# Three-layer graph convolution with residual and LayerNorm: VectorE's casts written as a maximum with a zero in PSUM, gathers of the later layers paced by TensorE, and some casts and waits moved

## The reference

```python
def conv(h, W, b):
    m = jnp.concatenate([h[dst], h[src], edge_attr], axis=1) @ W + b
    return jax.ops.segment_sum(m, dst, num_segments=n_nodes)
h = relu(conv(x, W1, b1)); h = relu(conv(h, W2, b2)); y = conv(h, W3, b3)
out = layernorm(x + y)
```

## Time and profile before

| | |
|---|---|
| three runs | 2799.05, 2801.68 (median), 2805.03 us |
| the profiled execution's own time | 2796.28 us |
| its span in the trace, mean granted TensorE clock | 2794.5 us, 0.981 |
| layer 0 (batches 0 to 24) | to about 1405 us of the span |
| batch 25 and the halves | about 1405 to 1453 us |
| layer 1 from batch 26, layer 2 | about 1453 to 2092 us, 2092 us to the end |

### The profile page before, as it was taken

How to read it: one execution, slowest core, us unless ns; L and a number is a source line. 1 busy time by engine, 2 the same in 40 slices (tenths; PEclk the granted TensorE clock), 3 DMA queues, 4 the chain that set the end, 5 groups by cost and what they waited for, 6 DMA issues and landing times.

```text
span 2794.5 us, 51850 instructions
## 1 busy us (share of the span) xinstructions
PE 2492.9 (89%) x18243; PEld 1820.8 (65%) x18243; DVE 2057.6 (74%) x4510; ACT 2171.0 (78%) x2972; POOL 1706.8 (61%) x1391
## 2 busy tenths in 40 slices
PE   1599999999999999999978888888887888888887
PEld 0155555556555555556657777877776777777777
DVE  7999999999999999999765555555553555555554
ACT  5799899898888988998517777777775777777776
POOL 5354454454453454554357777777766777777776
PEclk9699999999999999999989999999998999999999
DMA  4443533533534434434548777777775777777774
GB/s 94 126 149 113 180 125 113 189 115 122 179 116 137 167 113 153 151 113 174 193 128 270 250 250 248 244 250 252 246 239 183 246 237 246 237 236 242 241 241 127
DMA packets 257344, 519.32 MB, mean 186 GB/s; under 512 B 153954, under 2 KB 189784, under 8 KB 253889
## 3 DMA queue, kind: packets, MB, share of 16 engines
q1 hardware_dynamic: 152596, 299.50, 32.9%
q10 hardware_dynamic: 57404, 146.14, 13.9%
q0 software_dynamic: 47088, 70.34, 10.0%
HBM read 361.98 MB, written 153.81 MB: 185 GB/s over the span
## 4 chain that ended last, share of the span: by engine, by line
PE 49%; POOL 33%; issue 10%; DVE 5%; ACT 3%; DMA 1%; ACTq 0%; SPq 0%; DVEq 0%; POOLq 0%
POOL far_rows L895 32%; PE ps L1633 14%; PE ps L1604 14%; PE ps L1662 8%; PE ps L1648 3%; PE ps L1681 3%; ACT spread L1050 2%; PE ps L1734 2%; PE ps L1696 1%; PE ps L1699 1%; PE ps L1735 1%; DVE is_key L1274 1%; PE ps L1709 1%; ACT blocks L985 1%; PE ps L1720 1%
## 5 line engine op out<-in xcount | busy, mean ns | idle before, releaser
L895 POOL DMA_INDIRECT far_rows<-parts,far_src x1350 | 1652.2, 1224 | 1039.1 <-issue 368.3
L985 ACT ACTIVATE blocks<-ps 128x505 fp8e4<-128x505 f32 x1875 | 1117.8, 758 | 138.5 <-PE ps L1604 135.7
L1050 ACT CAST spread<-blocks 125x1500 fp32r<-125x1500 fp8e4 x637 | 897.6, 1443 | 250.3 <-PE ps L1648 229.0
L1515 DVE CAST spread<-blocks 125x1500 fp32r<-125x1500 fp8e4 x588 | 570.5, 974 | 606.0 <-PE ps L1648 603.0
L1604 PE MATMUL ps<-is_key,is_low 128*128 128x505 bf16 x1875 | 700.4, 384 | 31.4 <-DMA w_own<-in_L_gnn_W 13.9
L1633 PE MATMUL ps<-blocks,parts 125*128 125x375 fp8e4 x2600 | 719.1, 324 | 4.2 <-ACT blocks L985 2.4
L1274 DVE TENSOR_SCALAR is_key<-from_one,parts 128x500 bf16<-128x500 f16 x1875 | 614.9, 359 | 1.6 <-PE ps L1604 0.9
L1648 PE MATMUL ps<-spread,halves_last 125*128 125x376 f32 x2500 | 499.7, 347 | 87.5 <-ACT spread L1050 83.9
L1648 PEld LDWEIGHTS ps<-spread,halves_last 125*128 125x128 f32 x2500 | 422.5, 191 | 137.1 <-ACT spread L1050 128.1
L1633 PEld LDWEIGHTS ps<-blocks,parts 125*128 125x128 bf16 x2600 | 255.1, 99 | 191.7 <-issue 15.0
L1648 PE MATMUL ps<-spread,halves_kept 125*128 125x376 f32 x1440 | 285.7, 344 | 66.2 <-ACT spread L1050 48.1
(11 more groups left out here) (159 smaller groups left out, 1841.9 us busy)
## 6 DMA issues: line engine op xcount, KB each, us to landing
blocks<-counts SPq DMA_DIRECT2D x250, 937.5 KB, 5.0
counts<-blocks ACTq DMA_DIRECT2D x25, 4687.5 KB
far_rows<-parts,far_src POOLq DMA_INDIRECT x1350
far_masks<-far_masks_kept SPq DMA_DIRECT2D x50, 281.2 KB, 2.9
attr_stage<-in_edge_attr SPq DMA_DIRECT2D x125, 88.0 KB
far_masks_kept<-far_masks SPq DMA_DIRECT2D x25, 281.2 KB, 12.4
h_rows<-rows ACTq DMA_DIRECT2D x49, 128.0 KB
own_sb<-attr_sums ACTq DMA_DIRECT2D x49, 95.7 KB
```

The costliest lines, as they stand in the source:

```text
L895: nc.gpsimd.indirect_dma_start(far_rows[:, g % 2, j, 0:PARTS * D], None, parts_d[layer], bass.IndirectOffsetOnAxis(ap=far_src[:, g % BATCH ...
L985: nc.scalar.activation(blocks[:, b % 2, :, n * W:(n + 1) * W], build[:, c % BUILD, 0:COLS].rearrange("p (t w) -> p t w", w=W), ACT.Copy, s ...
L1050: nc.scalar.copy(spread[0:L, u % SPREAD_RING, :, 0:DENSE], counted(g, t, T)).then_inc(act_spread, 1)
L1515: nc.vector.tensor_copy(spread[0:L, u % SPREAD_RING, :, 0:DENSE], counted(g, t, T)).then_inc(dve_spread, 1)
```

## The change

Five edits.

1. VectorE's cast is a `tensor_tensor` maximum of the fp8 counts with one fp32 zero, read from PSUM (`zero_ps`, bank 1, cleared once) for every element. The result is the same fp32r.
2. Which engine casts which unit: `act_spreads(i)` gives ScalarE unit 19 too (`ACT_TOO`), so ScalarE casts 14 of 25 units and VectorE 11.
3. In layers 1 and 2 from batch 26 on, the gather j of batch g + 1 (j from 1) also waits until TensorE has used unit j * 25 // 18 - 1 of batch g. Batch 25's gathers are as before.
4. Order. VectorE casts the units of a fifth of batch 26 right after that fifth's halves, instead of all of them after all halves. ScalarE casts units 4 and 6 before `keep_h` (before only 4), and units up to 20 before `give_rows` (before up to 18). In layer 2 VectorE's cast amid `make_nodes` comes after the variance, and is that of unit 21.
5. In layer 0 `sum_far` does the low part with 64 columns of weights, even j to output partitions 0 to 63 and odd j to 64 to 127.

```diff
+    ACT_TOO = 19
...
+        def act_spreads(i):
+
+            return i % 2 == 0 or i == ACT_TOO
+
         def spreads_to(g, i):
...
+            mine = [k for k in range(FIFTHS * GROUP_OF) if act_spreads(k) == act_spreads(i)]
+            return (g - BATCHES - 1) * len(mine) + mine.index(i) + 1
...
+        zero_ps = ps[0:L, 1, 0:1]
...
                 if (g + 1) % BATCHES:
-                    gather_batch(g + 1)
+                    for j in range(FJ):
+                        if j:
+                            pool.wait_ge(spread_used, unit_at(g, j * (FIFTHS * GROUP_OF) // FJ - 1) + 1)
+                        gather_rows(g + 1, j)
...
                 keep_acc(g)
-                spread_act(h, 3, 5)
+                spread_act(h, 3, 7)
                 keep_h(g)
                 if g + 2 < ALL:
                     load_h(act, g + 2)
                 if h % BATCHES == 0 and h < ALL:
-                    spread_act(h, 5, 7)
                     give_rows(g)
...
                 else:
-                    spread_act(h, 5, 3 * m + 2)
+                    spread_act(h, 7, 3 * m + 2)
                     if g + 2 < ALL:
                         load_attr(act, g + 2)
-                    spread_act(h, 3 * m + 2, 3 * m + 4)
+                    rows_at = 3 * m + 6
+                    spread_act(h, 3 * m + 2, rows_at)
                     give_rows(g)
-                    spread_act(h, 3 * m + 4, FIFTHS * m)
+                    spread_act(h, rows_at, FIFTHS * m)
                     give_nodes(g)
...
                 ordered(nc.vector.tensor_reduce(mean[:, :], z[:, :, :], axis=X, op=ALU.add))
-                if amid:
-                    spread_dve(g + 1, amid, amid + 2)
...
                 nc.vector.tensor_reduce(var[:, :], left[:, :, :], axis=X, op=ALU.add).then_inc(var_ready, 1)
+                if amid:
+                    spread_dve(g + 1, amid, amid + 4)
...
-                    nc.vector.tensor_copy(spread[0:L, u % SPREAD_RING, :, 0:DENSE], counted(g, t, T)).then_inc(dve_spread, 1)
+                    nc.vector.tensor_tensor(spread[0:L, u % SPREAD_RING, :, 0:DENSE], counted(g, t, T),
+                                            zero_ps.rearrange("p (t s) -> p t s", t=1).to_broadcast([L, T, DENSE]), ALU.max
+                                            ).then_inc(dve_spread, 1)
...
+            first = units_of(BATCHES + 1)
             for q in range(FIFTHS):
                 halve(q)
-            spread_dve(BATCHES + 1, 0, 2)
+                spread_dve(BATCHES + 1, q * first, (q + 1) * first)
...
                 for j in range(FJ):
-                    last = nc.tensor.matmul(acc_ps(g, at), far_rows[:, g % 2, j, 2 * D:4 * D],
-                                            far_masks[:, g % 2, j, :], start=False, stop=(j == FJ - 1))
+                    if g < BATCHES:
+                        side = j % 2 * D
+                        last = nc.tensor.matmul(acc_ps(g, at)[side:side + D, :], far_rows[:, g % 2, j, 2 * D:3 * D],
+                                                far_masks[:, g % 2, j, :], start=False, stop=(j >= FJ - 2))
+                    else:
+                        last = nc.tensor.matmul(acc_ps(g, at), far_rows[:, g % 2, j, 2 * D:4 * D],
+                                                far_masks[:, g % 2, j, :], start=False, stop=(j == FJ - 1))
```

More of the change, by code:

```diff
@@ L1039, in spread_act @@
             def spread_act(g, first, stop):
-                for i in range(first + first % 2, min(stop, FIFTHS * units_of(g)), 2):
+                for i in range(first, min(stop, FIFTHS * units_of(g))):
+                    if not act_spreads(i):
+                        continue
                     u = unit_at(g, i)
                     t = batch_of(g, i) * T
-                    if i == 0 or batch_of(g, i - 2) // GROUP_OF != t // FIFTH:
+                    if i % GROUP_OF < 2:
                         wait_fifth(act, g, t)
@@ L1504, in spread_dve @@
             def spread_dve(g, first, stop):
-                for i in range(first + 1 - first % 2, min(stop, FIFTHS * units_of(g)), 2):
+                for i in range(first, min(stop, FIFTHS * units_of(g))):
+                    if act_spreads(i):
+                        continue
                     u = unit_at(g, i)
                     t = batch_of(g, i) * T
-                    if i == 1 or batch_of(g, i - 2) // GROUP_OF != t // FIFTH:
+                    if i % GROUP_OF < 2:
                         wait_fifth(dve, g, t)
@@ L1541, in _ @@
             dve.wait_ge(counts_stored[0], (BATCHES + 1) // 2 * DMA)
-            nc.vector.memset(spread[:, :, :, DENSE:WIDE].bitcast(fp32), 0.0).then_inc(spread_cleared, 1)
+            nc.vector.memset(spread[:, :, :, DENSE:WIDE].bitcast(fp32), 0.0)
+            ordered(nc.vector.memset(zero_ps, 0.0))
+            nc.vector.engine_nop().then_inc(spread_cleared, 1)
             dve.wait_ge(parts_stored[1], BATCHES * 2 * DMA)
+            first = units_of(BATCHES + 1)
             for q in range(FIFTHS):
                 halve(q)
-            spread_dve(BATCHES + 1, 0, 2)
+                spread_dve(BATCHES + 1, q * first, (q + 1) * first)
             for g in range(BATCHES, ALL):
@@ L1551, in _ @@
                 if g % BATCHES == 0:
-                    spread_dve(h, 3, 2 * m + 2)
                     if g == BATCHES:
                         find_bad()
-                    spread_dve(h, 2 * m + 2, FIFTHS * m)
+                    else:
+                        spread_dve(h, 3, FIFTHS * m)
                     spread_dve(h + 1, 0, 2)
@@ L1562, in _ @@
                     make_nodes(g, nodes_at)
-                    spread_dve(h, nodes_at + 2, FIFTHS * m)
+                    spread_dve(h, nodes_at + 4, FIFTHS * m)
                 else:
@@ L1644, in apply_split @@
                     pe.wait_ge(halved, i // units_of(g) + 1)
-                pe.wait_ge(dve_spread if i % 2 else act_spread, spreads_to(g, i))
+                pe.wait_ge(act_spread if act_spreads(i) else dve_spread, spreads_to(g, i))
                 rows = halves_of(layer, b)
@@ L1692, in sum_far @@
                 pe.wait_ge(far_landed[g % 2], (g // 2 + 1) * FJ * DMA)
-                if g == 0:
+                if g == BATCHES:
                     pe.wait_ge(zeros_ready, 1)
```

1 line of the change is left out of this document (added).

## The result

The changed kernel is faster: 2765.1 us median (2763.4 to 2767.3, four runs) against 2802.2 (2799.1 to 2805.0), a ratio of 0.9869 [0.9856, 0.9882]. A repeat on another chip gave 2764.6 against 2802.4, 0.9863 [0.9847, 0.9880]. The profiled execution took 2763.8 us, its span is 2762.0, against 2796.3 and 2794.5: 32.5 us to explain.

What follows compares the result with a forecast made beforehand. TensorE was taken to bound layer 0, gathers and the ring of casts side by side layers 1 and 2. -9.5 + 16 - 15 - 5 + 5 = -8.5 us, forecast 2793 us, range 2775 to 2813.

Steps and rivals of the forecast that it cites:

- The failed step: Layer 1, ScalarE's new order with VectorE's slower cast: a batch takes about 27.0 us, +0.73 in 22 batches, +16 us.
- Layer 0: Low pass of `sum_far` with matmuls on alternating halves: 0.38 us saved in each of 25 batches, -9.5 us.
- The cast: VectorE's two-operand cast with an operand in PSUM takes 1.72 us, bounds 0.97 and 1.85.
- the other estimate, 1.69: VectorE's new cast by the Trainium skill's 120 cycles plus one an element at 0.96 GHz; sum about 4 us lower.
- The gathers: Layers 1 and 2: a gather takes 1.04 us beside the new cast, 24.1 us a batch with 0.30 more each.
- Layer 2 and the step between the layers: Layer 2 without ScalarE's wait for VectorE's variance, -15 us; faster gathers between layers 1 and 2, -5 us.
- Batch 26: VectorE's casts between the halves: unit 3's cast waits for unit 0 and holds the other halves, +5 us.
- Layer 1 doesn't pay: Rival: ScalarE's casts of 19 and 20 hide in TensorE's order, layer 1 keeps 26.4 us; -24 us, 2777 us; chance 0.13.
- Gathers stay slow: Rival: something other than the casts slows gathers, layer 2 stays at 26.9, the boundary gains nothing; 2813 us; chance 0.12.

## Why the prediction was wrong

**The failed step** is the term "Together a batch is 26.30 - 0.19 + 0.87, about 27.0 us", +16 us for layer 1. Its 7.18 us, from the end of cast 18 to that of cast 24, hold "`give_rows` in layer 1 stands for 1.69". In the changed order it stands for 0.87, and the trace has 6.33 us in the place of 7.18. Two smaller errors stand beside it. The 6.31 of before has the 1.69 of the one batch in it; in the mean it was 6.16. And cast 18 ends 0.30 us earlier after the last `sum_far` than before (19.10 us after its start for 19.40), not 0.19. So a batch changed by -0.30 + 6.33 - 6.16 = -0.13 us where I had +0.68: -2.9 us in 22 batches, and with the 1.0 of the first batch the -3.9 that were measured. Both ends of the term, +6 and +24, were on the wrong side; the lower one had the stores "partly hidden", while the wait for the parts and the whole issue of the stores went. I had treated the same thing rightly in layer 2, where the wait for the variance had a row of its own. In layer 1 the wait was inside a gap put down to TensorE.

**Layer 0**: -8.5 for -9.5 at batch 24, and the copy comes once in 51.14 us ((1309.4 - 235.5) / 21, from its 22 copies up to that time) for 51.55: right.

**The cast**: 1.715 us for 1.72. The figure rests on a line through two rows of other shapes and operands, so that it came within 0.01 is partly luck; the other estimate, 1.69, was nearly as near.

**The gathers**: the direction and the cause were right, the size not: 0.955 us for 1.04. The stretch of rows 7 that I took it from had VectorE's work on the halves beside it, which has operations with two operands in SBUF; that these slow a gather too is argued from the run with the zero in SBUF. It changes nothing in the sum, since 1.04 didn't bind.

**Layer 2 and the step between the layers**: -18.8 and -6.2 for -15 and -5; the wait for the variance is gone and no gather is waited for in layer 2.

**Batch 26**: +4.7 for +5. Its two causes go together: from `sum_far` of batch 24 to that of 26 it takes 76.0 us before, 77.7 with the new cast in the old order, 74.2 with the old cast in the new order, and 80.7 with both. So "the edit that is to overlap halves with matmuls costs" holds only with the slow cast, and what this edit costs by itself stays open, since it wasn't undone alone on a chip of the first kind.

**The rivals**: "Layer 1 doesn't pay", 2777 us, was nearest, but for another reason than that casts 19 and 20 hide. "Gathers stay slow" didn't happen; the run with the zero in SBUF shows what it would have looked like.

The sum with -3 for +16 would have been -27.5 from the profiled execution, 2769; measured were 2763.8.

## What to carry to other kernels

A gap on an engine between two instructions is a price only once each part of it is found working, and in more batches than one: look on the engine's own DMA queue and on the producers for something that ends just before the gap does, for the row of the gap names one releaser and the wait may belong to an instruction in between. Moving such a step behind more work can make it free, and its place can be worth several per cent. Two parts of a change that lose or give nothing alone (2946 and 2806 us for 2802) can gain together (2765), so an order and the durations in it are to be tried together; and an edit worth nothing on one chip can be worth a fifth of the time on another.

## What the runs showed of the hardware

- A maximum with a zero in PSUM leaves a gather at 0.95 us, the same with the zero in SBUF 1.39, the one-operand cast 1.16 to 1.21 (a gather's time, us); mixes lie between (1.11 with six old casts of eleven, 1.04 in layer 1 with five of eleven).
- ScalarE's DMA issues ran ahead of its casts: the two stores were issued at 1655.48, in the middle of casts that ended at 1656.85. But an issue that still waited held the casts behind it: 1.49 us for 0.87 with late parts, and 0.83 us a batch behind `load_attr`.
- The granted clock was 0.93 in layer 1 with `give_rows` early, where TensorE was busy for 86% of the time, and 1.00 in the changed kernel, with 90%.
- Chips of one type differ: the kernel before takes 2800 to 2802 us on some, and 2877 to 2887 on others, and unpaced bursts of fast gathers cost 659 us on one of the second kind and nothing on one of the first.
